# Four batch norm coefficient stages of a one-core convolution network folded into the heads of the stages that use them

## The reference, cut to what matters

```python
# layer 1: spectral convolution (DFT by matmul, complex mix, inverse DFT) + bias
# layer 2: graph convolution, ends with
mean = jnp.mean(y, axis=(0, 2, 3), keepdims=True)
var = jnp.var(y, axis=(0, 2, 3), keepdims=True)
y = (y - mean) * lax.rsqrt(var + BN_EPS)
return jax.nn.relu(y * gamma[None, :, None, None] + beta[None, :, None, None])
# layer 3: deformable ("snake") convolution; its two offset branches are each
h = conv2d(x, dw_w, dw_b, padding=1, groups=x.shape[1])     # depthwise
h = jax.nn.relu(batchnorm(h, bn_g, bn_b))                   # batch norm
return conv2d(h, pw_w, pw_b, padding=0)                     # pointwise: the offsets
# ... and its output is relu(batchnorm(fused, fus_bn_g, fus_bn_b))
# layer 4: 3x3 convolution with averaged transformed kernels
```

## Time and profile before

| | |
|---|---|
| three runs, median | 4675.08 us (4657.65 to 4681.07) |
| the profiled execution, its own time | 4662.39 us |
| its span, first to last instruction | 4660.3 us |
| what lies around the span | 2.1 us |
| TensorE busy | 3750.7 us (80%), mean granted clock 0.889 |
| VectorE / ScalarE / GpSimd busy | 2683.8 / 2206.1 / 1472.7 us |

### The profile page before, as it was taken

One profiled execution on the slowest core, in us unless ns is written; L12 is line 12 of the kernel. 1 busy time (PEld: TensorE's weight loads), 2 busy tenths in 40 slices (PEclk: granted clock), 3 DMA queues, 4 the chain that ended last, 5 costly groups with the idle time before them and its releaser, 6 DMA issues. The chain is left out here.

```text
span 4660.3 us, 152910 instructions
## 1 busy us (share of the span) xinstructions
PE 3750.7 (80%) x63427; PEld 2350.2 (50%) x63427; DVE 2683.8 (58%) x4309; ACT 2206.1 (47%) x2870; POOL 1472.7 (32%) x1450
## 2 busy tenths in 40 slices
PE   6765558434999977299999999999999999990388
PEld 5665445332343322056666666666666666660133
DVE  4303646442333345467878777787877878784411
ACT  5500114232222234167777777777777777771111
POOL 0001210011000012155656565565656556550000
PEclk9955659766999988699999999999999999995699
DMA  3265659998787757312122121221212122119766
GB/s 93 67 132 143 177 116 255 232 345 201 214 225 208 217 197 267 108 54 75 51 60 66 49 83 50 72 59 51 68 55 73 55 72 60 41 50 287 216 189 176
DMA packets 804820, 606.68 MB, mean 130 GB/s; under 512 B 65992, under 2 KB 727112, under 8 KB 795756
## 3 DMA queue, kind: packets, MB, share of 16 engines
q1 hardware_dynamic: 652424, 442.79, 35.9%
q10 hardware_dynamic: 141840, 121.83, 8.4%
q0 software_dynamic: 9984, 33.56, 2.2%
HBM read 383.31 MB, written 214.70 MB: 128 GB/s over the span
## 5 line engine op out<-in xcount | busy, mean ns | idle before, releaser
L1547 DVE TENSOR_SCALAR df_t<-df_d 128x1024 f32<-128x1024 f32 x1024 | 1248.1, 1219 | 258.6 <-PE df_d L1618 255.5
L1527 ACT ACTIVATE df_t<-df_a 128x1024 f32<-128x1024 f32 x1024 | 1048.1, 1024 | 683.8 <-PE df_a L1618 683.8
L1473 POOL TENSOR_SCALAR df_t<-df_t 128x1024 f32<-128x1024 f32 x1024 | 1064.5, 1040 | 925.3 <-ACT df_t L1527 925.3
L1670 PE MATMUL df_o<-df_t,df_zs 128*32 128x128 f32 x36864 | 1220.5, 276 | 0.5 <-DVE df_u L1565 0.5
L1670 PEld LDWEIGHTS df_o<-df_t,df_zs 128*32 128x32 f32 x36864 | 945.2, 110 | 393.6 <-issue 355.6
L1651 PE MATMUL df_z<-df_wz,df_x 32*128 32x288 f32 x4096 | 774.7, 454 | 6.1 <-POOL df_x L1493 5.8
L1533 ACT ACTIVATE df_zs<-df_z 128x576 f32<-128x576 f32 x1024 | 661.2, 646 | 7.3 <-PE df_z L1651 7.3
L1618 PE MATMUL df_a<-df_ix,net_sel 7*128 7x512 bf16 (+1 forms) x2048 | 504.1, 383 | 0.6 <-DVE df_zt L1580 0.6
L1618 PE MATMUL df_d<-df_ix,net_sel 7*128 7x512 bf16 (+1 forms) x2048 | 491.1, 379 | 0.0
L1553 DVE TENSOR_SCALAR df_t<-df_s 128x512 f32<-128x512 f32 x512 | 354.1, 692 | 140.4 <-PE df_s L1618 140.4
L1651 PEld LDWEIGHTS df_z<-df_wz,df_x 32*128 32x128 f32 x4096 | 307.4, 183 | 87.6 <-ACT df_zs L1533 66.8
(11 more groups left out here) (224 smaller groups left out, 4398.9 us busy)
## 6 DMA issues: line engine op xcount, KB each, us to landing
r_x<-x SPq DMA_DIRECT2D x64, 512.0 KB, 14.2
x<-r_x ACTq DMA_DIRECT2D x64, 512.0 KB, 11.4
gc_x<-x SPq DMA_DIRECT2D x240, 128.0 KB, 5.0
dc_x<-x SPq DMA_DIRECT2D x240, 128.0 KB, 3.2
dc_xt<-x_2t SPq DMA_DIRECT2D x240, 128.0 KB, 4.6
lc_x<-x SPq DMA_DIRECT2D x112, 256.0 KB, 4.6
fw_x<-in_x SPq DMA_DIRECT2D x32, 512.0 KB, 6.7
iv_x<-in_x SPq DMA_DIRECT2D x64, 256.0 KB, 4.7
```

Of the source, the lines that this page charges most:

```text
L1473: g.tensor_scalar(t, t, 1.0, 0.0, ALU.min, ALU.max).then_inc(clipped, 1)
L1527: act.activation(t, ps_a[:], ACT.Relu).then_inc(a_read, 1)
L1547: v.tensor_scalar(t, ps_d[:], 0.0, 1.0, ALU.max, ALU.min).then_inc(d_read, 1)
L1670: mm = pe.matmul(ps_o[32 * q:32 * q + 32, 0:P], Zs[:, n % 2, q, 32 * k:32 * k + 32], T[:, n % 2, slot(k), P * q:P * q + P], start=(start a ...
```

## The change

`norm_coefficients` and its four blocks go. A class `Coefficients` takes its place: it holds the tiles and one PSUM bank, and gives each engine the same instructions to put at the head of its own list in another stage's block. `residual_norm` makes one ("r1" for n1, "r2" for nf), `offsets` two (nx, then ny). On ScalarE they stand behind the semaphore increments at the head of `residual_norm`, and end with a new wait until scale and bias are written. The last VectorE instruction now raises the semaphore too (10 steps a call for 9). The loads of SyncE have no new wait.

```diff
-def norm_coefficients(nc, sems, name, turn, st, parts, share, gb, out):
...
+class Coefficients:
+    STEPS = 10
+    def __init__(self, s, name, turn, st, share, gb, out):
...
+        self.ps = s.ps(name + "ps", [P, 512])
+        self.ready = self.STEPS * (turn + 1)
+    def vector(self, v):
...
+        ch = Chain(v, self.sems.steps, self.STEPS * self.turn)
+        ch.done(v.bn_aggr(ag[:], self.st[:].rearrange("p n s -> p (n s)")))
+        v.wait_ge(sums, 2 * self.turn + 1)
+        ch.done(v.tensor_copy(cs[:, 0:1], ps[:, 0:1]))
...
+        v.wait_ge(rooted, self.turn + 1)
+        ch.done(v.reciprocal(cs[:, 1:2], cs[:, 1:2]))
...
+        ch.done(v.tensor_tensor(out[:, 1:2], gb[:, 1:2], cs[:, 2:3], ALU.subtract))
+    def tensor(self, pe):
+        S0 = self.STEPS * self.turn
+        pe.wait_ge(self.sems.steps, S0 + 1)
+        pe.matmul(self.ps[:, 0:1], self.share, self.ag[:, 0:1], start=True, stop=True).then_inc(self.sems.sums, 1)
+        pe.wait_ge(self.sems.steps, S0 + 5)
+        pe.matmul(self.ps[:, 1:2], self.share, self.dev[:], start=True, stop=True).then_inc(self.sems.sums, 1)
+    def scalar(self, a):
+        a.wait_ge(self.sems.steps, self.STEPS * self.turn + 6)
+        a.activation(self.cs[:, 1:2], self.cs[:, 1:2], ACT.Sqrt).then_inc(self.sems.rooted, 1)
+        a.wait_ge(self.sems.steps, self.ready)
...
-def residual_norm(nc, sems, name, y, coef, x, x_out, pair, GS, turn=None):
+def residual_norm(nc, sems, name, y, norm, coef, x, x_out, pair, GS, turn=None):
...
+        co = Coefficients(s, "co", *norm, coef)
...
+                co.scalar(a)
                 with a.Fori(0, B // NS) as i:
...
+                co.vector(v)
                 v.sem_inc(steps, 2)
...
+                co.tensor(pe)
                 pe.wait_ge(c_in, 16)
...
-def offsets(nc, sems, hx, hy, cox, coy, wt, off, edge):
+def offsets(nc, sems, hx, hy, normx, normy, cox, coy, wt, off, edge):
...
+        norms = [Coefficients(s, "cx", *normx, cox), Coefficients(s, "cy", *normy, coy)]
...
+                for co in norms:
+                    co.scalar(a)
                 rectify(0, 0)
...
+                for co in norms:
+                    co.tensor(pe)
                 for n in range(NT):
...
+                for co in norms:
+                    co.vector(v)
                 for n in range(NT + 2):
...
-        norm_coefficients(nc, sems, "n1", 0, st1, P, wt["share"][:], wt["gb1"], co1)
-        norm_coefficients(nc, sems, "nx", 1, stx, P, wt["share"][:], wt["gbx"], cox)
-        norm_coefficients(nc, sems, "ny", 2, sty, P, wt["share"][:], wt["gby"], coy)
-    norm_coefficients(nc, sems, "nf", 3, stf, P, wt["share"][:], wt["gbf"], cof)
```

More of the change, by code:

```diff
@@ new lines @@
+class Coefficients:
+    STEPS = 10
+    def __init__(self, s, name, turn, st, share, gb, out):
+        self.sems, self.turn, self.st, self.share, self.gb, self.out = s.sems, turn, st, share, gb, out
+        self.ag, self.dev, self.cs = s.sb(name + "ag", [P, 2]), s.sb(name + "dev", [P, 1]), s.sb(name + "cs", [P, 3])
+        self.ps = s.ps(name + "ps", [P, 512])
+        self.ready = self.STEPS * (turn + 1)
+    def vector(self, v):
+        ag, dev, cs, ps, out, gb = self.ag, self.dev, self.cs, self.ps, self.out, self.gb
+        sums, rooted = self.sems.sums, self.sems.rooted
+        ch = Chain(v, self.sems.steps, self.STEPS * self.turn)
+        ch.done(v.bn_aggr(ag[:], self.st[:].rearrange("p n s -> p (n s)")))
+        v.wait_ge(sums, 2 * self.turn + 1)
+        ch.done(v.tensor_copy(cs[:, 0:1], ps[:, 0:1]))
+        ch.sync()
+        ch.done(v.tensor_tensor(dev[:], ag[:, 0:1], cs[:, 0:1], ALU.subtract))
+        ch.sync()
+        ch.done(v.tensor_tensor(dev[:], dev[:], dev[:], ALU.mult))
+        ch.sync()
+        ch.done(v.tensor_tensor(dev[:], dev[:], ag[:, 1:2], ALU.add))
+        v.wait_ge(sums, 2 * self.turn + 2)
+        ch.done(v.tensor_scalar(cs[:, 1:2], ps[:, 1:2], EPS, None, ALU.add))
+        v.wait_ge(rooted, self.turn + 1)
+        ch.done(v.reciprocal(cs[:, 1:2], cs[:, 1:2]))
+        ch.sync()
+        ch.done(v.tensor_tensor(out[:, 0:1], cs[:, 1:2], gb[:, 0:1], ALU.mult))
+        ch.sync()
+        ch.done(v.tensor_tensor(cs[:, 2:3], cs[:, 0:1], out[:, 0:1], ALU.mult))
+        ch.sync()
+        ch.done(v.tensor_tensor(out[:, 1:2], gb[:, 1:2], cs[:, 2:3], ALU.subtract))
+        assert ch.n == self.STEPS
+    def tensor(self, pe):
[8 more added lines that the diff above has]
+        a.wait_ge(self.sems.steps, self.ready)
@@ L1870, in layer_rest @@
         graph_conv(nc, sems, x1, gstat, wt, d, y1, st1)
-        norm_coefficients(nc, sems, "n1", 0, st1, P, wt["share"][:], wt["gb1"], co1)
-        residual_norm(nc, sems, "r1", y1.rearrange("b p j n -> b p (j n)"), co1, mod4(x1), mod4(x2), d["pair"], GS, (xt, wt["eye"][:]))
+        residual_norm(nc, sems, "r1", y1.rearrange("b p j n -> b p (j n)"), (0, st1, wt["share"][:], wt["gb1"]), co1, mod4(x1), mod4(x2), d["pair"], GS, (xt, wt["eye"][:]))
         depth_conv(nc, sems, x2, xt, GS, wt, hx, hy, up, stx, sty)
-        norm_coefficients(nc, sems, "nx", 1, stx, P, wt["share"][:], wt["gbx"], cox)
-        norm_coefficients(nc, sems, "ny", 2, sty, P, wt["share"][:], wt["gby"], coy)
-        offsets(nc, sems, hx, hy, cox, coy, wt, off, edge)
+        offsets(nc, sems, hx, hy, (1, stx, wt["share"][:], wt["gbx"]), (2, sty, wt["share"][:], wt["gby"]), cox, coy, wt, off, edge)
     deformable(nc, sems, (mod4(xt), mod4(x2)), GS, up, off, edge, z0d, wt, uy, u, stf)
-    norm_coefficients(nc, sems, "nf", 3, stf, P, wt["share"][:], wt["gbf"], cof)
-    residual_norm(nc, sems, "r2", u.rearrange("b q o h w -> b (q o) (h w)"), cof, mod4(x2), mod4(x3), d["pair"], GS)
+    residual_norm(nc, sems, "r2", u.rearrange("b q o h w -> b (q o) (h w)"), (3, stf, wt["share"][:], wt["gbf"]), cof, mod4(x2), mod4(x3), d["pair"], GS)
     last_conv(nc, sems, x3, GS, wt["L3"], wt["pick"][:], out)
```

## The result

Over 14 runs each, the changed kernel took 4650.72 us (4635.5 to 4666.57) and the kernel before 4666.58 us (4655.84 to 4688.17). The ratio is 0.9959, with a 95% interval of 0.9946 to 0.9972: 19 us less, between 13 and 25. The forecast was 22.0 us, 0.47%. Three remarks on reading it. The ratio is not that of the two medians, which stand 15.9 us apart; the means, 4668.8 and 4650.2, stand 18.6 apart. The median of before was 8.5 us lower over 14 runs than over the three that the prediction started from, and the gain was smaller than forecast; the two errors offset each other in part, so that the absolute 4653.1 came within 2.4 us of the result by luck. And one profile against one profile would have misled: the spans are 4660.3 and 4656.2 us, 4.1 us apart.

A forecast was written before the change was run, and what follows sets the result against it. Bound taken: strictly ordered stages, with coefficient blocks as latency chains while DMA queues are empty. Earlier loads gain 21.72 us, plus 0.1 three times: 22.0; other terms zero. Median 4675.08 - 22.0 = 4653.1 us, range 4636 to 4670.

The forecast's parts named there:

- The blocks go: At the starts of r1, offsets and r2, first loads issue 5.41, 10.88 and 5.43 us earlier; 22.0 us gained in all.
- Nothing is paid for the move: In r1, offsets and r2, coefficient chains end before the loads land; cost zero, narrowest slack 2.2 us at offsets.
- the upper bound of 5.79: Longest expected time in us of one moved chain, from r2's per-image chain with stores under way; lower bound 5.16.
- Table switch: ScalarE, square root then ReLU in the changed stages: 0 to 0.78 us, taken as 0; 2.66 us if tables change.
- ScalarE's wait: New wait until scale and bias are written, ahead of the first ReLU; holds no load back, cost nought.
- Clock, 0 within 4 us: TensorE's granted clock may rise at another time behind the three changed stage starts; bounds -4 and +4 us, taken 0.
- Rival A: Engines start late at the starts of r1, offsets and r2: 10.8 us lost, gain 11.2, time 4663.9; chance 0.10.
- B: Coefficients late at offsets because DMA traffic stretches the chain, 2.9 us past the loads: gain 19.1, time 4656.0; chance 0.05.
- the cover: Wait for first loads that hides the moved coefficients: 21.55 us in r1, 12.57 in offsets, 20.58 in r2.
- C: Slower through deformable, whose code moves address: 43 ns a step eats the gain, 86 ns gives 4697 us; chance 0.04.
- D: More than the sum: TensorE's clock rises earlier behind the three changed stage starts, 4 us more, time 4649; chance 0.05.
- a stage behind a head longer than before: Sign of being wrong: a stage takes longer after its opening wait for loads in r1, offsets or r2; no size given.

The follow-up runs named there:

- held: Changed kernel, but SyncE waits for the coefficients ahead of its first load in both residual_norm stages and offsets; ratio to before 0.9991 (0.9977 to 1.0005).
- eight: Kernel before with each of the four coefficient stages run three times in a row, eight blocks more; ratio to before 1.0105 (1.0091 to 1.0119).
- late1: Changed kernel with one more bn_aggr, result unused, ahead of the two coefficient chains in offsets; ratio to before 0.9952 (0.9935 to 0.9968).
- of_only: Kernel before with only the two coefficient blocks ahead of offsets folded in, those of residual_norm kept as stages; ratio to before 0.9986 (0.9969 to 1.0004).
- late5: Changed kernel with five more bn_aggr, results unused, ahead of the two coefficient chains in offsets; ratio to before 0.9980 (0.9965 to 0.9996).

## Why the prediction was right

*The blocks go (22.0 us).* Right: 21.8 us at the heads, SyncE's first issue within 0.1 us of the meeting, the four waits gone. "held" shows it as a cause and "eight" gives the price, 6.1 us a block by the time (5.3 to 7.0) for 5.4 in the timeline.

*Nothing is paid for the move.* Right. The chain took 5.16 us beside the loads (872.94 to 878.10, DMA share 0.64), not a hundredth more than in the quiet block; the pair took 10.29 at a share of 0.92 for the 10.32 of the sum, and 2.16 us were left for the 2.2. So the upper bound of 5.79, read from the loop's chain, was no effect of traffic, and the choice of the lower end was right. That the loop's own instructions make up the 0.63 us, the reason given, was not tested; the timelines show that it lies in the hand-overs between engines (0.07 to 0.17 us more at each of six), and none of it in VectorE's steps.

*Table switch, ScalarE's wait.* Nought, as put. The trace of before could have settled the first, as it has no table load behind 1.0 us.

*Clock, 0 within 4 us.* Not separated from the rest of a stage's scatter. In `depth_conv`, 15 to 35 us behind its start, the granted clock was 0.80 in both profiles of before and 0.87 and 0.86 in both of the changed kernel, which by (0.87 - 0.80) x 20 is an estimated 1.4 us; but it was 0.80 in "late1" and 0.87 in "of_only" too, so it doesn't follow the change.

*Rival A* (late starts at the heads) didn't occur: the meetings are followed by the first issue in under 0.1 us, though the coefficient blocks no longer stand in between. *B*: the cover held; it fails from 2.2 us of extra work, as "late5" shows. *C*: `deformable` took 2265.7 us before and 2266.0 after; TensorE by stretch shows it as steady as in the earlier trace rows:

```profile
2100.00:2600.00 500.00, 494.42 (x11413) 1.00 0.22 62
3600.00:4100.00 500.00, 493.43 (x11364) 1.00 0.21 58
```

*D*, 4 us more than the sum, didn't occur: the gain came out under the sum.

*The total.* 19 us measured (13 to 25) for 22. The 3 us between lie inside the interval. One sign that the prediction named for being wrong did show, "a stage behind a head longer than before", and one for being right did not: over the two profiles of each kernel `last_conv` started 8 to 14 us earlier, not 22. Much of this can be the scatter of stages, to which the prediction gave no size, but it can't be told apart from a loss. If the 3 us are real, the table points to the rest of "r2", and the step that would be at fault is the silent one, that behind the heads nothing changes; the means there are 0.3, 1.1 and 3.5 us longer. No run settled it. The change stayed within 0.5%, the likeliest outcome by the prediction, for the reason given: even the full gain is worth less than that.

## What to carry to other kernels

Where stages are closed by a meeting of all engines, ask of each small stage which engine or queue has nothing in it, and what that engine could already do for the next stage. The gain is the small stage's whole length as long as its chain is shorter than the wait that it moves beside, and the slack between the two is the number to keep, for it is also how much the head can be shortened by other means before the chain shows. And where the gain is about as large as the scatter of the runs, multiply the effect (three blocks for one) rather than the runs.

## What the runs showed of the hardware

Small VectorE and TensorE instructions were not slowed by loads beside them: ten of the one and two matmuls of the other took 5.16 us in all at a DMA share of 0.01 and at 0.64 alike, and two such chains took 10.29 us at 0.92. Stages differ between executions of the same work: "r2", where the DMA share is 1.0, took 166.8 to 175.9 us, and `last_conv`, with TensorE busy for 80% and a granted clock of 0.92 to 0.96, took 286.0 to 296.9. `deformable`, eight times as long, with TensorE busy for 96% at 0.98 to 0.99, stayed within 2.2 us (2265.2 to 2267.4). A single pair of profiles can so hide four fifths of a real gain.
